# Layer attention: four PSUM banks for the rows, two for the scores, one maximum instruction for the two heads of a part

## The reference

```python
def _attn(x, W_qkv, b_qkv, W_ao, b_ao):
    b, s, d = x.shape
    qkv = jnp.einsum('bsd,od->bso', x, W_qkv) + b_qkv
    qkv = qkv.reshape(b, s, 3, H, DH)
    q = jnp.moveaxis(qkv[:, :, 0], 2, 1)
    k = jnp.moveaxis(qkv[:, :, 1], 2, 1)
    v = jnp.moveaxis(qkv[:, :, 2], 2, 1)
    scores = jnp.einsum('bhqd,bhkd->bhqk', q, k) * SCALE
    wts = jax.nn.softmax(scores, axis=-1)
    o = jnp.einsum('bhqk,bhkd->bhqd', wts, v)
    o = jnp.moveaxis(o, 1, 2).reshape(b, s, d)
    return jnp.einsum('bsd,od->bso', o, W_ao) + b_ao
```

## Time and profile before

| | us |
|---|---|
| median of 3 runs | 3271.56 |
| lowest and highest | 3259.83, 3273.29 |
| the profiled execution's own time | 3267.46 |
| its span, first to last instruction | 3265.8 |
| busy: PE | 2812.3 (86%) |
| busy: DVE | 1863.4 (57%) |
| busy: ACT | 1770.7 (54%) |
| busy: POOL | 805.1 (25%) |

### The profile page before, as it was taken

The page is one execution under the profiler, slowest core; times in us unless marked ns, Lnnn a source line. Parts: engine busy times, 40 slices in busy tenths (PEclk is TensorE's granted clock), DMA queues, the critical chain, the costliest instruction groups (busy, mean ns, idle before and its releaser), DMA issues.

```text
span 3265.8 us, 56810 instructions
## 1 busy us (share of the span) xinstructions
PE 2812.3 (86%) x17396; PEld 1737.5 (53%) x17396; DVE 1863.4 (57%) x3116; ACT 1770.7 (54%) x2669; POOL 805.1 (25%) x864
## 2 busy tenths in 40 slices
PE   7877799787899787898788879999966999799999
PEld 4444446444455444464444446666644777466666
DVE  4567735577546577445677345444536887454444
ACT  6457656367655377654477654444422666544443
POOL 0212200122100222101122014444440000244444
PEclk8989999799899699999799989999987999899999
DMA  2134300244200344101344000000002332000000
GB/s 94 43 94 108 79 6 8 67 100 107 52 12 8 89 103 104 26 8 33 93 99 98 6 7 1 0 0 0 0 1 94 98 101 72 4 4 7 3 6 6
DMA packets 95850, 150.50 MB, mean 46 GB/s; under 512 B 13152, under 2 KB 81248, under 8 KB 89312
## 3 DMA queue, kind: packets, MB, share of 16 engines
q1 hardware_dynamic: 95712, 148.77, 17.3%
HBM read 79.00 MB, written 67.11 MB: 45 GB/s over the span
## 4 chain that ended last, share of the span: by engine, by line
PE 43%; issue 23%; DVE 13%; POOL 11%; DMA 4%; SPq 2%; ACT 2%; DVEq 1%; POOLq 1%; ACTq 0%
POOL hhlo L2179 9%; DVE hmx L1849 9%; PE ps L948 7%; PE ps L754 3%; PE ps L973 2%; PE ps L717 2%; PE ps L681 2%; PE ps L687 2%; PE ps L793 2%; PE ps L829 2%; PE ps L1154 1%; DMA hqk<-hqk_scratch 1%; PE ps L815 1%; SPq L556 1%; DMA hqk_scratch<-hqks 1%
## 5 line engine op out<-in xcount | busy, mean ns | idle before, releaser
L1849 DVE TENSOR_REDUCE hmx<-ps 128x2 f32<-128x512 f32 x1024 | 660.1, 687 | 310.9 <-PE ps L948 310.1
L1445 ACT ACTIVATE hpt<-ps 128x1024 f32<-128x1024 f32 x512 | 522.3, 1024 | 289.5 <-PE ps L960 287.7
L2179 POOL TENSOR_TENSOR hhlo<-hh,hhh 128x512 fp32r<-128x512 f32 x320 | 414.8, 1296 | 463.0 <-ACT hhh L1524 462.1
L948 PE MATMUL ps<-hqk 24*128 24x256 f32 x2048 | 309.0, 359 | 235.1 <-DVE hmx L1849 189.1
L948 PEld LDWEIGHTS ps<-hqk 24*128 24x128 f32 x2048 | 191.5, 206 | 461.8 <-DVE hmx L1849 412.1
L1519 ACT ACTIVATE sil<-ps 128x512 f32<-128x512 f32 x320 | 191.0, 597 | 441.4 <-PE ps L1156 437.4
L1943 DVE TENSOR_TENSOR su<-ps,sil 128x512 f32<-128x512 f32 x256 | 177.1, 692 | 326.7 <-PE ps L1156 318.4
L973 PE MATMUL ps<-hpt,hvx 128*32 128x256 f32 x4096 | 299.3, 413 | 1.9 <-ACT hpt L1445 1.6
L960 PE MATMUL ps<-hqk 26*128 26x256 f32 x2048 | 272.2, 348 | 1.7 <-ACT hpt L1445 1.2
L1524 ACT ACTIVATE hhh<-hh 128x512 fp32r<-128x512 f32 x320 | 199.5, 624 | 40.9 <-DVE hh L1946 26.8
L2136 POOL CAST hqks<-hqk 128x512 fp32r<-128x512 f32 x64 | 40.5, 633 | 673.3 <-ACT hqk L1425 641.8
(11 more groups left out here) (247 smaller groups left out, 5593.1 us busy)
## 6 DMA issues: line engine op xcount, KB each, us to landing
hqk_scratch<-hqks SPq DMA_DIRECT2D x256, 192.0 KB, 3.1
hqk<-hqk_scratch SPq DMA_DIRECT2D x256, 192.0 KB
qk_scratch<-qks SPq DMA_DIRECT2D x16, 768.0 KB, 3.3
k<-qk_scratch SPq DMA_DIRECT2D x16, 384.0 KB
qv<-qk_scratch SPq DMA_DIRECT2D x64, 96.0 KB
mw<-mw_in SPq DMA_DIRECT2D x10, 516.5 KB, 3.9
w12raw<-w_in SPq DMA_DIRECT2D x1, 2560.0 KB, 9.5
streams<-x_in SPq DMA_DIRECT2D x8, 256.0 KB, 4.8
```

Of the source, the lines that this page charges most:

```text
L948: return mm(ps[:, o % 2, qt * SEQ:(qt + 1) * SEQ], hqk[r][32 * g:32 * g + 24, 0, j, qt * P:(qt + 1) * P], hqk[r][32 * g:32 * g + 24, 1, j, ...
L1445: A(hpt[:, j, g:g + 2, :, :], ps[:, 2 + g:4 + g, :], ACT.Exp, scale=QSCALE).then_inc(hd_exp, 1)
L1849: V.tensor_reduce(hmx[:, r, :, 4 * g + j], ps[:, o % 2, :].rearrange("p (t k) -> p t k", t=2), AX.X, ALU.max).then_inc(hd_max, 1)
L2179: G_.tensor_tensor(hhlo[:, k % 4, :], hh[:, k % 2, :], hhh[:, k % 4, :].bitcast(F32), ALU.subtract).then_inc(e_lo, 1)
```

## The change

Rows get four banks, 0 to 3 (`o % 4`), scores two, 4 and 5, the same two for every part. PE waits at the head of a part for the exponential of the part before instead of two parts ago (line 1013) and for the maxima of two parts ago instead of one (line 1015). DVE reduces the rows of both heads of a part with one instruction over two banks (128x1024 in, 128x4 out), after the second head's rows are there, and adds 2 to `hd_max`. The rows before sequence 0 go in the same pairs.

```diff
--- before.py
+++ after.py
@@ -945,19 +945,19 @@
                 def row(o, r, qt):
 
                     j, g = ORDER[o] // 4, ORDER[o] % 4
-                    return mm(ps[:, o % 2, qt * SEQ:(qt + 1) * SEQ],
+                    return mm(ps[:, o % 4, qt * SEQ:(qt + 1) * SEQ],
                               hqk[r][32 * g:32 * g + 24, 0, j, qt * P:(qt + 1) * P],
                               hqk[r][32 * g:32 * g + 24, 1, j, :], start=True, stop=True)
 
                 def rows(b, o, r):
-                    pe.wait_ge(hd_max, nth(hd_max, l * BATCH + b, o - 2))
+                    pe.wait_ge(hd_max, nth(hd_max, l * BATCH + b, o - 4))
                     row(o, r, 0)
                     row(o, r, 1).then_inc(hd_am, 1)
 
                 def score(s, r, kt):
 
                     j, g = s // 4, s % 4
-                    return mm(ps[:, 2 + g, kt * SEQ:(kt + 1) * SEQ],
+                    return mm(ps[:, 4 + g % 2, kt * SEQ:(kt + 1) * SEQ],
                               hqk[r][32 * g:32 * g + 26, 1, j, kt * P:(kt + 1) * P],
                               hqk[r][32 * g:32 * g + 26, 0, j, :], start=True, stop=True)
 
@@ -1010,9 +1010,9 @@
                             pe.wait_ge(hd_scat, every(hd_scat, B + 2))
                         ahead, o, ra = (1, 8 + 2 * p, (r + 1) % 4) if p < 4 else (2, 2 * p - 8, (r + 2) % 4)
                         both = n1 if p < 4 else n2
-                        pe.wait_ge(hd_exp, nth(hd_exp, B, p - 2))
+                        pe.wait_ge(hd_exp, nth(hd_exp, B, p - 1))
                         if both:
-                            pe.wait_ge(hd_max, nth(hd_max, B + ahead, o - 1))
+                            pe.wait_ge(hd_max, nth(hd_max, B + ahead, o - 3))
                         for t in range(2):
                             if both:
                                 for u in range(2):
@@ -1442,7 +1442,7 @@
                     j, g = p // 2, 2 * (p % 2)
                     act.wait_ge(hd_sc, nth(hd_sc, B, p))
                     act.wait_ge(hd_pv, nth(hd_pv, B - 1, j))
-                    A(hpt[:, j, g:g + 2, :, :], ps[:, 2 + g:4 + g, :], ACT.Exp, scale=QSCALE).then_inc(hd_exp, 1)
+                    A(hpt[:, j, g:g + 2, :, :], ps[:, 4:6, :], ACT.Exp, scale=QSCALE).then_inc(hd_exp, 1)
 
                 def raw(b):
                     B = l * BATCH + b
@@ -1843,11 +1843,13 @@
 
             def head_attention(l, part="middle"):
                 def maxima(b, o, r):
+
                     B = l * BATCH + b
                     j, g = ORDER[o] // 4, ORDER[o] % 4
-                    dve.wait_ge(hd_am, nth(hd_am, B, o))
-                    V.tensor_reduce(hmx[:, r, :, 4 * g + j], ps[:, o % 2, :].rearrange("p (t k) -> p t k", t=2), AX.X,
-                                    ALU.max).then_inc(hd_max, 1)
+                    dve.wait_ge(hd_am, nth(hd_am, B, o + 1))
+                    V.tensor_reduce(hmx[:, r].rearrange("p t (g j) -> p g j t", g=GROUPS)[:, g:g + 2, j, :],
+                                    ps[:, o % 4:o % 4 + 2, :].rearrange("p u (t k) -> p u t k", t=2), AX.X, ALU.max)\
+                     .then_inc(hd_max, 2)
 
                 def minus_max(b, r):
 
@@ -1870,7 +1872,6 @@
                         ahead, o, ra = (1, 8 + 2 * p, (r + 1) % 4) if p < 4 else (2, 2 * p - 8, (r + 2) % 4)
                         if n1 if p < 4 else n2:
                             maxima(b + ahead, o, ra)
-                            maxima(b + ahead, o + 1, ra)
                         if p == 3 and n1:
                             minus_max(b + 1, (r + 1) % 4)
                         if p == 7 and not first:
@@ -1879,10 +1880,10 @@
                 if part == "end":
                     return [lambda: add_out(15)]
 
-                for o in range(HEADS):
+                for o in range(0, HEADS, 2):
                     maxima(0, o, 0)
                 minus_max(0, 0)
-                for o in range(8):
+                for o in range(0, 8, 2):
                     maxima(1, o, 1)
                 heads(dve, step, lambda: None)
```

## The result

| | before | changed |
|---|---|---|
| median of 11 runs, us | 3263.61 | 3280.29 |
| lowest to highest | 3252.89 to 3273.29 | 3273.47 to 3294.77 |
| the profiled execution's own time | 3267.46 | 3294.77 |

The changed kernel takes 1.0049 times as long, interval 1.0034 to 1.0063: half a per cent slower, where 0.8% faster was forecast, and 13 us above the upper end of the range. Its profiled execution is the slowest of its eleven, 27.3 us above the profiled one of before where the medians are 16.7 apart; it is used for what happens within a stage, and totals are taken from the ratios.

A forecast was written before the change was run, and what follows sets the result against it. The prediction took the kernel to be bound by TensorE and VectorE waiting for each other over two row banks. Its terms, -43 + 11 + 6 = -26 us against 3267.5, gave 3241 us, range 3213 to 3267.

The forecast's parts named there:

- What bounds the kernel before, and what the change frees: Row loop: TensorE and VectorE wait for each other, 1.88 us a part, 15.47 a sequence; four row banks open it.
- One maximum instruction, 1.22 us, worth nothing: VectorE's maximum for two heads: eight take 9.8 us a sequence, off the path, so no gain or cost by itself.
- The DMA of the maxima: Before part 0 of a sequence: issued behind the spill, it lands 0.13 to 0.2 us late, making 14.6 a sequence.
- The new wait: Head of each part: scores wait for the previous exponential, return to TensorE 0.06 us; 1.77 into even parts, 1.70 into odd.
- The interval of the reciprocals, 2.23: Between exponentials 4 and 5: ScalarE's reciprocals make this interval 2.23 us, longer than the ordinary part.
- my loop of 14.5: Sum of a sequence's eight exponential-to-exponential intervals through TensorE and ScalarE, without the DMA wait: 14.5 us.
- The last sequence: Last sequence of each layer, no rows: 10.8 us becomes 13.5, loss 11 us in four layers, plus 6 for the clock.
- How many sequences gain: Sequences 0 to 13 of four stages: 49.7 at full clock gain 0.87 us each, 43 us in all.
- Rival (a): TensorE's clock falls in further parts and takes the gain; with 60 such parts about 3295 us; chance 0.10.
- Start of a layer, nothing: First rows of a layer: four banks speed them, but the first part waits for a DMA; no gain, at most 2 us.
- Rival (b): The maxima's DMA before part 0 becomes the bound; 0.5 us later costs 25 us: 3266, no change; chance 0.16.
- (d): The pair maximum takes above 1.7 us, so VectorE stays the bound: 3284 us; chance 0.02.

The follow-up runs named there:

- its experiment: Changed kernel, but parts without rows put odd parts' scores in banks 2 and 3, waiting for the exponential two parts back: 3255.07 us, ratio 0.9955.

## Why the prediction was wrong

*What bounds the kernel before, and what the change frees:* right. The maxima left the chain; the spacing fell by 0.44 us, since the loop through VectorE was cut.

*One maximum instruction, 1.22 us, worth nothing:* right for the changed banks (1225 ns; no difference with two). My aside that it costs nothing by itself was too general: on banks 0 and 1 it costs 0.03 us a part.

*The steps that failed*, in the terms of the sum: the gain of 43 us in sequences 0 to 13 was too large, since the DMA wait and TensorE's return were too small in it and the clock's part was put at nothing; and the 17 us of the last sequences were 25. The rest of this section takes them one by one.

*The DMA of the maxima:* right in mechanism, too small, and it is the step that set the spacing. By its own chain the forecast was 1.70 + 1.77 from exponential 0 to 2, 10.48 from there to the next part 0, and 0.69 to its exponential: 14.6. Measured it is 1.75 + 1.83 (278.22 to 281.80), 292.54 - 281.80 = 10.74, and 0.68: 15.0. Of the 0.26 us of the middle term 0.16 are between the end of the spill's last issue and the first of the maxima (0.19, where I put 0.03), 0.07 ahead of it and 0.03 behind it. So part 0 waits 0.33 us rather than 0.13 to 0.2. With the waits exchanged it stands 0.65 us beyond the return (335.88 to 336.53), and the spacing is still 14.88.

*The new wait, term "from its end back to TensorE 0.06":* wrong. I took the return from rows where the exponential's wait is the last before the matmuls; in the changed part a register operation and a second wait stand behind it. It is 0.13 to 0.14. The diff shows this order, and in the earlier trace rows the wait that ended last was the last in order: the step could have been made. Beside the DMA it is worth only the 0.11 us up to exponential 2; where no DMA hides it, 0.48 us a sequence.

*The interval of the reciprocals, 2.23:* misread, and it hid part of the wrong return. In the earlier trace rows exponential 5 starts 0.62 us after part 5, and the odd parts of the changed kernel have 0.60 (282.96 to 283.56): it waited for TensorE's scores and not for ScalarE. Between exponentials 4 and 5 the changed kernel has 287.49 - 285.40 = 2.09:

```profile
286.95 0.63 ACT L1459 ACTIVATE hrec<-hrec 128x512 f32<-128x512 f32 x1
287.49 1.01 ACT L1445 ACTIVATE hpt<-ps 128x1024 f32<-128x1024 f32 x1
```

ScalarE's exponential follows the reciprocal's line by 0.54 us here; before it followed by 0.69:

```profile
315.26 0.63 ACT L1459 ACTIVATE hrec<-hrec 128x512 f32<-128x512 f32 x1
```

With six returns of 0.07 us more my loop of 14.5 would have been 14.9; measured without its DMA wait it is 15.00 - 0.33 = 14.67, and 14.71 in the kernel with the projections earlier and the old wait order. With the return as I counted it, it is 14.23, 0.3 below my sum. That the 14.5 lies so near to 14.67 is luck.

*The last sequence:* the loss of 2.7 us a layer at full clock was right in kind: its parts without other work of ScalarE come 1.60 to 1.62 apart at full clock, 1.62 counted. The clock's part was the mis-sized term. I took 1.5 us of a bound of 5; sequence 15 went from 9.9 to 16.1 us on average, 6.2 more, so 3.5 for the clock. With 25 us instead of 17 in the four layers it is the largest single loss, and 31 us by its experiment.

*How many sequences gain:* I counted 49.7 sequences at the clock of before. In sequences 0 to 13 the profile has 160 us at half clock instead of 123, and the granted clock fell to 0.89 in one stage, where I had "not below 0.91". Fifty-six sequences at the full-clock spacings would take 866 us before and 841 after; the profiles have 892 and 891. So the stretches at half clock cost 26 us before and 50 after, and this took the whole gain of 25; the execution with two maxima, the same in all else, kept 10 us of it (881 us). Rival (a) came in part. Its counter-argument, that the load is denser, did not hold: the clock fell more often all the same.

*Where the clock fell:* counted in the traces' records, in sequences 0 to 12, it fell 18 times in the changed kernel, 14 of them just as part 1 began, behind the part 0 that waits for the DMA. The other four kernels of this layout with that wait have 11 to 20 falls. In the kernel that sends the maxima before the last spill there are 8, only one of them at part 1 and six around part 4, where TensorE waits in that kernel. The three kernels of this layout that have no DMA wait in sequences 1 to 12 have 4, 2 and 2. So in the changed layout the falls go with the DMA waits. It is no rule for both: the five kernels with the banks of before, where part 0 waits for the DMA in at most 6 of the 48 sequences 1 to 12, have 10 to 18. Each count is of one execution, and what makes the clock fall there stays open.

*Start of a layer, nothing:* right. From the end of one stage to the first exponential of the next it is 214 to 216 us in both profiles.

*Rival (b)* named the right place, *(d)* did not happen. Against the kernel before, the profiles have 1 us less in sequences 0 to 13 where 43 less were forecast, and 25 us more in the last sequences where 17 were; the other executions, at a granted clock of 0.922 to 0.928 instead of 0.920, lost less. The range, 3213 to 3267, left out (a), and its own bounds for the clock of the last sequences, +15, and for the DMA added up to more than it allowed.

## What to carry to other kernels

Before pricing a new wait, read in which order the waits stand and what is issued between them: the one that ends last belongs last. When a loop is shortened, walk each chain that is tied to one of its steps, DMA issues included, and compare its length with the new loop; here a DMA wait of 0.8 us gave way to one of 1.2 when only its own DMA was moved, and only moving their common start removed both. And price the parts of a schedule that lack the usual work, first and last, by themselves: here the eight parts without rows in each layer cost more, 25 to 31 us, than the fifty-odd sequences gained by their spacing.

## What the runs showed of the hardware

- A register operation and a second, long satisfied wait behind the wait that ends last cost TensorE 0.07 to 0.08 us: 0.14 against 0.06 in the changed kernel, 1.95 against 1.88 a part in the kernel before.
- Two DMAs of 16 KB issued directly behind four of 192 KB were waited for until 3.01 to 3.04 us after the first of them was issued. An issue of spill or maxima held SyncE's queue some 0.6 us, one of the scatter 0.3 to 0.4.
- A small VectorE operation with two SBUF inputs took 0.76 us where GpSimd's operation had started some 0.01 us before it, and 0.19 us where GpSimd's started at most 0.006 us before it, after it, or not during it.
- A shorter loop did not by itself mean a steadier or a less steady clock: spacings of 15.46, 15.02 and 14.23 us had 123, 160 and 88 us at half clock in the same 56 sequences, and a second kernel with a spacing of 14.23 had 135. In the changed layout the clock fell 11 to 20 times in sequences 0 to 12 with a DMA wait at part 0, and 2 to 4 times with none in sequences 1 to 12.
